# One TensorE signal per pair of pages in the expert stage, with the transposes two pairs ahead of their products

## The reference

```
x = x + LN(attn(LN(x)))        # 4 heads of 64, keys and queries RMS-normalised
x = x + LN(ffn(LN(x)))         # ffn(y) = y + expert_w[argmax(gate(y))] @ y, 8 experts
```

## Time and profile before

| | us |
|---|---|
| median of three runs | 691.83 |
| the profiled execution | 692.4 |
| its span | 690.5 |
| products of pair 0 begin | 613.20 |
| products of pair 4 begin | 629.23 |
| products of pair 19 begin | 677.46 |
| GpSimd issues the last page | 684.18 |

### The profile page before, as it was taken

How to read it: one execution, slowest core, us unless ns; L and a number is a source line. 1 busy time by engine, 2 the same in 40 slices (tenths; PEclk the granted TensorE clock), 3 DMA queues, 4 the chain that set the end, 5 groups by cost and what they waited for, 6 DMA issues and landing times. The chain is left out here.

```text
span 690.5 us, 21513 instructions
## 1 busy us (share of the span) xinstructions
PE 607.0 (88%) x8717; PEld 424.9 (62%) x8717; DVE 573.5 (83%) x1115; ACT 534.2 (77%) x848; POOL 262.1 (38%) x422
## 2 busy tenths in 40 slices
PE   4899789999999999877898799999999997568880
PEld 2677446666666667755775366666666676446760
DVE  5999778998889889899987689887888898976762
ACT  4798878898889899765888798888888897445642
POOL 3344444333333332003677333333323320555563
PEclk9999999999999999999999999999999999979995
DMA  5941299889888996121222989898988963228120
GB/s 168 296 124 30 58 173 180 169 153 183 168 166 156 183 170 135 61 84 46 62 71 72 183 146 164 154 168 154 164 162 156 164 129 108 70 75 302 65 73 32
DMA packets 60664, 92.87 MB, mean 134 GB/s; under 512 B 7057, under 2 KB 29844, under 8 KB 60566
## 3 DMA queue, kind: packets, MB, share of 16 engines
q0 software_dynamic: 35088, 66.13, 49.9%
q1 hardware_dynamic: 24902, 25.37, 12.7%
q10 hardware_dynamic: 576, 0.00, 0.0%
HBM read 15.87 MB, written 14.66 MB: 44 GB/s over the span
## 5 line engine op out<-in xcount | busy, mean ns | idle before, releaser
L693 ACT ACTIVATE e_f<-banks,nbias,c_ 128x1024 f32<-128x1024 f32 x172 | 200.8, 1202 | 44.1 <-PE banks L1571 31.1
L1571 PE MATMUL banks<-qk_T 128*128 128x512 f16 (+1 forms) x1024 | 217.4, 384 | 12.2 <-ACT qk_T L631 4.8
L1615 PE MATMUL banks<-v_mm,e_l 128*128 128x65 f16 x2048 | 201.6, 193 | 0.0
L1615 PEld LDWEIGHTS banks<-v_mm,e_l 128*128 128x128 f16 x2048 | 185.9, 97 | 0.0
L1123 DVE TENSOR_TENSOR e_l<-e_f,e_h 128x1024 f16<-128x1024 f32 x100 | 120.3, 1224 | 22.1 <-DMA e_h<-e_f 16.4
L1613 PE MATMUL banks<-v_mm,e_h 128*128 128x65 f16 x1184 | 117.9, 194 | 1.9 <-DVE e_l L1123 1.3
L1614 PE MATMUL banks<-v_lo,e_h 128*128 128x64 f16 x1184 | 117.9, 192 | 0.0
L1613 PEld LDWEIGHTS banks<-v_mm,e_h 128*128 128x128 f16 x1184 | 108.0, 97 | 14.7 <-issue 2.6
L1571 PEld LDWEIGHTS banks<-qk_T 128*128 128x128 f16 (+1 forms) x1024 | 51.0, 96 | 103.6 <-issue 62.2
L1614 PEld LDWEIGHTS banks<-v_lo,e_h 128*128 128x128 f16 x1184 | 107.5, 99 | 9.6
L693 ACT ACTIVATE x_all<-banks,nbias,c_ 128x1024 f32<-128x1024 f32 x84 | 98.8, 1200 | 6.9 <-DVE e_l L1123 6.2
(11 more groups left out here) (294 smaller groups left out, 1250.6 us busy)
## 6 DMA issues: line engine op xcount, KB each, us to landing
e_h<-e_f POOLq DMA_DIRECT2D x86, 256.0 KB, 4.0
e_x<-e_f POOLq DMA_DIRECT2D x62, 256.0 KB, 3.8
e_h<-x_all POOLq DMA_DIRECT2D x42, 256.0 KB, 4.2
e_x<-x_all POOLq DMA_DIRECT2D x30, 256.0 KB, 4.6
x_all<-x SPq DMA_DIRECT2D x12, 512.0 KB, 4.3
rows_d<-e_x SPq DMA_DIRECT2D x1, 5180.0 KB, 24.5
qk_T<-rows_d SPq DMA_DIRECT2D x20, 259.0 KB, 6.1
qk_T<-qk_T SPq DMA_DIRECT2D x16, 256.0 KB, 4.8
```

The source lines that it names most:

```text
L693: act.activation(whole[s % ALL % NEF], ps_S[s % ALL % 3], ACT.Exp, bias=bias_of(h, k // NT), scale=CESC).then_inc(s_E, 1)
L1571: return pe.matmul(ps_S[s % ALL % 3][:, c * BANK:(c + 1) * BANK], k_T[rows, 1 - c if cross else c, h * N + j * P:h * N + (j + 1) * P], q_T ...
L1615: ins = pe.matmul(o, low[s % ALL % NLO][:, at], v[:, 0:DH + 1], start=False, stop=j == NT - 1, skip_group_check=True)
```

## The change

The last transpose of a pair no longer increments `s_TX`, except for the pairs 0, 1, 4 and 5 (`OPENING`), whose transposes stand ahead of all products of their part. Only the last matmul of a pair increments `s_U`, so it counts pairs and not pages. The transposes stand one pair further ahead: TensorE's order is now `rows_T(q + 2)`, `expert(q)`, `keep_running(2)`. The signal of `expert(q)` therefore says two things: the products of pair q are there, and so is the turned pair q + 2. `high_rows(q + 2)` and `u_squares(q)` on ScalarE wait for the same count. VectorE's `low_rows` and `base` move one pair forward accordingly. The matmuls, their number and their sizes are the same. The increments of `s_U` fall from 39 to 20 and those of `s_TX` from 20 to 4.

```
@@ tables
+    OPENING = [0, 1, EARLY, EARLY + 1]
@@ ScalarE
             def high_rows(q):
                 at = q % 2 * 2 * P
-                act.wait_ge(s_TX, q + 1)
-                if 2 * (q - 1) > 0:
-                    act.wait_ge(s_U, 2 * (q - 1))
+                if q in OPENING:
+                    act.wait_ge(s_TX, OPENING.index(q) + 1)
+                if q >= 2:
+                    act.wait_ge(s_U, q - 1)
...
             def u_squares(q):
-                act.wait_ge(s_U, 2 * q + tiles(q))
+                act.wait_ge(s_U, q + 1)
...
             for q in range(NPR):
-                if 0 < q < NPR - 1 and q + 1 != EARLY:
-                    high_rows(q + 1)
                 if act_bases(q):
                     second_base(q)
+                if q + 2 < NPR and q + 2 not in OPENING:
+                    high_rows(q + 2)
                 u_squares(q)
                 u_root(q)
                 if q + 1 == EARLY:
                     high_rows(EARLY)
+                    high_rows(EARLY + 1)
@@ VectorE
             base(1)
+            low_rows(2)
             finish(0)
             table_marks()
-            low_rows(2)
             base(2)
+            low_rows(3)
             finish(1)
             table_sums()
-            low_rows(3)
...
             low_rows(EARLY)
+            low_rows(EARLY + 1)
             for q in range(EARLY, NPR):
-                if q == EARLY + 1:
-                    base(q)
-                    finish(q - 1)
                 if q + 1 < NPR:
-                    low_rows(q + 1)
-                if q > EARLY + 1:
-                    base(q)
-                    finish(q - 1)
-            finish(NPR - 1)
+                    base(q + 1)
+                if q + 2 < NPR:
+                    low_rows(q + 2)
+                finish(q)
@@ TensorE
-                ins.then_inc(s_TX, 1)
+                if q in OPENING:
+                    ins.then_inc(s_TX, 1)
...
                 for t, w in enumerate(first):
                     at = (q % 2 * 2 + t) * P
-                    products(...).then_inc(s_U, 1)
+                    ins = products(...)
+                ins.then_inc(s_U, 1)
...
                     rows_T(q)
-                if 0 < q < NPR - 1 and q + 1 != EARLY:
                     rows_T(q + 1)
-                if q == EARLY:
                     keep_running(3)
+                if q + 2 < NPR and q + 2 not in OPENING:
+                    rows_T(q + 2)
                 if q % AHEAD == 0:
                     loaded = offsets(q)
                 expert(q, loaded[...])
```

More of the change, by code:

```diff
@@ L1489, in expert @@
                     at = (q % 2 * 2 + t) * P
-                    products(ps_U[q % NU][:, t, :], [(a[:, k, at:at + P], e[:, k, bass.ds(w, D)])
-                                                     for a, e in ((y_h, we_h), (y_l, we_h), (y_h, we_l)) for k in range(KH)]).then_inc(s_U, 1)
+                    ins = products(ps_U[q % NU][:, t, :], [(a[:, k, at:at + P], e[:, k, bass.ds(w, D)])
+                                                           for a, e in ((y_h, we_h), (y_l, we_h), (y_h, we_l)) for k in range(KH)])
+                ins.then_inc(s_U, 1)
             for b in range(0, NB):
```

## The result

The changed kernel is slower. Four runs of it took 698.46 to 701.16 us, median 700.59; four runs of the kernel before beside them had a median of 692.61. The ratio is 1.0088, with a 95% interval of 1.0054 to 1.0122. Forecast were 683.5 us and a range of 680.0 to 691.5: the time lies above the range, and the sign is wrong. The profiled execution took 698.46 us, its span is 696.7, 6.2 more than before. The medians lie 7.98 apart, so these two traces hold 6.2 us of the loss, not all of it.

A forecast was written before the change was run, and what follows sets the result against it. The prediction took GpSimd's back-to-back page writes, which hold TensorE's signals, to bound the expert stage. Opening +0.7, loop -7.7 and end -1.3 gave -8.3 us on the 691.83 median: 683.5 us, range 680.0 to 691.5.

The forecast's parts named there:

- The opening: Pairs 0 to 3, ahead of the loop: transposes moved earlier and squares moved behind the copy cost +0.7 us together.
- Squares behind the copy: ScalarE: u_squares(q) behind high_rows(q + 2) delays pages up to 0.60 us; taken as +0.3 us (bounds -2.0 to +0.8).
- Transposes earlier: TensorE: rows_T(6) ahead of pair 4's products waits for low_rows(4), +0.36 us once; the other moves keep the count.
- The loop: Pairs 4 to 19: 15 pairs at 2.70 us, 40.5 in place of 48.23, so -7.7 us (bounds -9.5 to +9.2).
- L: One hold, a TensorE signal's lateness, added to 3.50 us per two pairs in the loop; mean taken as 2.19 us.
- 2.70: Forecast us per pair in the loop, taken between GpSimd's 2.58 and the 2.85 that a 2.19 us hold gives.
- R4: Rival: each pair's one signal held 4.15 us, pairs at 3.83, +9.9 us, 701.7 us; chance 0.08.
- The end: From pair 19's products to the last page: at least one queued page gone without the stall, -1.3 us (bounds 0, -3.5).
- The cause of the stalls: Expert stage: TensorE's signals are held while GpSimd issues indirect DMAs back to back, so TensorE stops; 3.22 us per pair.
- Added waits: ScalarE's shared count and VectorE's base(q + 1) ahead of low_rows(q + 2), waiting for an older page, cost nothing.
- R3: Rival: signal count does not matter; stall comes with time or another event like the offsets load; 692.5 us, chance 0.13.
- R1: Rival: GpSimd alone sets the pace, holds stay short, 2.58 us per pair, -11.4 us, 680.4 us; chance 0.20.

The follow-up runs named there:

- before_third: The kernel before, unchanged, executed once for its trace on a chip where no signal is held: 680.50 us.
- after_third: The changed kernel, unchanged, on a chip where no signal is held: 681.44 us, ratio 1.0023 to the kernel before.
- late_two: The changed kernel with the order of the kernel before for pairs 0 to 3: 695.80 us, ratio 1.0053 to the kernel before.
- the second pair of traces: Traces of before_again and after_again, both kernels unchanged: 693.27 us for the single execution of the former, median 699.08 us for the latter.
- one_signal: The kernel before in its own order, with one signal per pair for the products, transposes still signalling: 693.10 us, ratio 0.9981 to the kernel before.
- half_before_2: The kernel before without the write of each pair's second page (output incomplete), on a chip that holds signals: 675.13 us, ratio 0.9753 to the kernel before.
- paced_before_2: The kernel before with four matmuls in place of two behind each pair's products: 695.43 us, ratio 1.0048 to the kernel before.
- before_again: The kernel before, unchanged, executed once for its trace: 693.27 us.
- after_again: The changed kernel, unchanged, run again on another occasion: 699.08 us, ratio 1.0057 to the kernel before.

## Why the prediction was wrong

**The opening, +0.7 forecast. From the base of pair 0 to pair 4 it grew by 2.40 and 5.31 us where signals are held, by 3.45 on a free chip.** Pair 4 itself began 3.33, 5.98 and 2.33 us later; the difference is how early the base of pair 0 started in that execution. before_third and after_third show the opening without any hold. ScalarE in before_third: the base of pair 0, whose start marks the same point in both, and the squares of pair 0:

```profile
613.38 0.59 ACT L568 ACTIVATE e_l<-qk_T 128x256 f32<-128x256 f32 x1
613.92 0.39 ACT L556 ACTIVATE e_f<-banks 128x256 f32<-128x256 f32 x1
```

ScalarE in after_third, the base, the copy of pair 2, the squares of pair 0:

```profile
612.26 0.59 ACT L570 ACTIVATE e_l<-qk_T 128x256 f32<-128x256 f32 x1
615.24 0.60 ACT L551 ACTIVATE y_h<-banks 128x512 fp32r<-128x512 f32 x1 [2.40 <-PE banks L1365]
615.74 0.38 ACT L558 ACTIVATE e_f<-banks 128x256 f32<-128x256 f32 x1
```

TensorE in after_third, transposes of pair 2, products of pair 0, then the dummies that wait for the offsets table, transposes of pair 6 and products of pair 4:

```profile
611.11 1.09 PE L1474 MATMUL banks<-ident,qk_T 128*128 128x128 f32 x4 [2.86 <-DVE y_l L885]
612.28 0.79 PE L1365 MATMUL banks<-we_h,y_h 128*128 x2
...
625.15 1.90 PE L1463 MATMUL banks<-ident 128*128 128x512 f16 x8 [2.41 <-DVE eoff L921]
...
628.99 0.63 PE L1474 MATMUL banks<-ident,qk_T 128*128 128x128 f32 x4 [0.42 <-DVE y_l L885]
629.87 0.50 PE L1365 MATMUL banks<-we_h,y_h 128*128 x2 [0.25 <-issue]
```

From the base to the squares of pair 0 are 0.54 us before and 3.48 after. Three things add up. The transposes of pair 2 now stand ahead of the products of pair 0 and wait for the same low part; I had written of pair 6 alone, and that the other moves keep the count. Those transposes (1.09 us for four, 0.60 in the earlier trace rows) and the products (0.79 for the first two, 0.50 in before_third) ran at 1.2 GHz (granted clock 0.50) after 2.86 us of idle time, where before_third had 2.4 GHz (1.00) after 1.80 us; that part is not the change's alone, as the last section shows. And the squares stand behind a copy that waits for the products. The table is made behind `finish(0)` on VectorE, so TensorE waits 2.41 us for it, which it did not before. I had priced *Squares behind the copy* at the copy's own length and halved it; the price is the wait that stands in front of the copy. *Transposes earlier*, 0.36 for pair 6, was 1.15 in late_two. The measured growth of 2.4 to 5.3 us lies far above my bound of +0.8. How it divides between the three, and how much of it is the clock, no run separates.

**The loop, -7.7 forecast, +2.6 measured from pair 4 to pair 19, +2.5 for the 31 pages** (+2.3 and +2.2 in the second pair of traces). The failing step is the use of L: I took a hold as a delay of 2.19 us on the mean that every pair pays once and that shrinks when fewer signals queue, and put the balance at 2.70 us per pair, 40.5 in all. Measured are 683.40 - 632.56 = 50.84 us, 3.39 per pair. It is not an even delay: four signals that ScalarE was waiting for were late, by 5.0, 2.0, 4.1 and 5.0 us, and the others that it waited for came within 0.04 us. The sample was too small as well: the trace before has products that ended at 670.38 and were read at 674.54, 4.16 us late, which I did not count, and by R4's own sum the loop decides from 2.93 on. And one_signal gives no sign that the count matters.

What the runs show in its place: GpSimd's pages come in longer runs, and it waits longer between them. Before, they come in runs of 2, 2, 6, 2, 6, 2, 4, 2 and 5 pages, with 8 waits; after, in runs of 6, 6, 6, 8 and 5, with 4 waits of 4.43, 2.91, 3.03 and 4.79 us. The long holds end near the end of a run. So I read it like this: two pairs of look-ahead lengthen the supply of pages that are ready, and with it the run that holds a signal; TensorE still runs out of work during the hold, and the cycle begins again. That a longer run makes a longer hold is argued and not shown: after runs of 6 the holds were 5.0, 2.0 and 4.1 us, and in one_signal the 6.9 us fell beside a run of 6 and, 0.53 us behind it, one of 2. The 2.70 had a second fault: I let GpSimd's 2.58 us bound the start of TensorE's pairs. In before_third, where nothing is held and GpSimd writes almost without a break, they start (662.18 - 627.54) / 15 = 2.31 us apart, and the queue of pages takes up the difference.

**The end, -1.3 forecast.** Pair 19 now begins 690.33 - 683.40 = 6.93 us ahead of the last page, where it was 6.72. The stall in front of pair 19 stayed (4.24 us, 4.33 before), so nothing was gained.

**What held.** The cause of the stalls, TensorE's signals beside writes in a row, was read rightly from the earlier trace rows as far as half_before_2 can tell. *Added waits* cost nothing on VectorE. R3 had the count right, as far as the noise lets one see, and the offsets load wrong. R4 was the rival that came true in its time, 701.7 against 700.6, but by luck: it put +0.7 into the opening and +9.2 into the loop at an even pace of 3.83, where the trace has +2.40 and +2.61 at 3.39 on the mean, in stretches at 2.30 with stalls between them. Its hold of 4.15 us was nearly met or passed by three of the four late signals (4.1, 5.0 and 5.0). I had argued against it that GpSimd would be idle for 1.2 us in each pair. It is idle in one piece behind the stall instead. R1's picture, pages that only GpSimd paces, is what a free chip shows.

## What to carry to other kernels

When a signal is late because another engine is busy, ask how long that engine stays busy before you count signals: here more look-ahead went with longer runs of the very work beside which signals were late, and with longer waits. When a step is moved ahead of another on an in-order engine, price the wait that it brings with it, at the first turn of the loop too, where nothing is queued that could hide it. And compare a change on more than one chip before its mechanism is settled.

## What the runs showed of the hardware that was not expected

- The same kernel had medians of 691.9 to 694.0 us in three comparisons and of 679.8 to 680.4 in three others, which ran on other chips. Most of the difference stands in the 31 pages, 50.3 and 51.3 us in traces of the first kind and 40.28 in one of the second. In none of the ten traces from chips of the second kind does ScalarE, from 580 us on, have a wait that ends with "remote"; what makes the chips differ is open.
- Where signals are held beside indirect writes that are 1.29 us apart, the four late ones of the trace after arrived 2.19, 0.66, 0.78 and 2.54 us behind the start of a run's last write, and one in paced_before_2 2.1 us. With one write per pair and gaps of 0.9 us or more none was late.
- TensorE's clock at the start of pair 0 is not fixed by the idle time ahead of it. In both of these traces it ran dummies and then stood idle. In before_again it did nothing for 1.72 us and then had the full 2.4 GHz (granted clock 1.00), in after_again for 1.61 us and had 1.2 GHz (0.50). The stretch from 612 to 615 us (columns as in the earlier trace rows), first before_again, then after_again:

```profile
612.00:615.00 3.00, 1.28 (x11) 1.27 (x11) 2.93 (x11) 1.40 (x4) 1.95 (x2) 1.00 0.12 44
```

```profile
612.00:615.00 3.00, 1.39 (x5) 0.62 (x4) 2.83 (x13) 0.73 (x2) 1.66 (x2) 0.50 0.12 44
```
